# Loading the first batch's state ahead of the weights, and summing it later on VectorE

## The reference

```
# layer 0: cross attention over channels; x_c = x, x_s = context
Mn = Wn @ inorm(x_c) + bn ;  Mm = Wm @ inorm(x_s) + bm
A  = softmax(Mn^T Mm)            # 512 x 512 per batch
x  = Wo @ ((Wl @ x_s + bl) A^T) + bo + x_c
# layer 1: a recurrent block over 128 time steps, 32 heads of 16, state = context
xa = layernorm(x) ; sx = shifted(xa, state row 1) - xa
five mixes of xa and sx -> k, w, v, r, g
s0 = state[:, 2:2+16]            # 32 heads x 16 x 16, the start of the recurrence
out_t = r_t (u * k_t v_t + s) ;  s = k_t v_t + w_t * s
groupnorm(out) * g @ Wo.T + x -> layernorm -> gated feed-forward
```

## Time and profile before

| | us |
|---|---|
| time, median of 3 runs | 1791.22 (1788.71 to 1792.86) |
| time of the execution that was profiled | 1793.89 |
| its span in the trace | 1792.1 |
| PE busy | 1701.1 (95%) |
| DVE busy | 1666.4 (93%) |
| ACT busy | 1183.9 (66%) |
| POOL busy | 1071.3 (60%) |
| mean granted TensorE clock | 0.978 |

### The profile page before, as it was taken

One profiled execution on the slowest core, in us unless ns is written; L12 is line 12 of the kernel. 1 busy time (PEld: TensorE's weight loads), 2 busy tenths in 40 slices (PEclk: granted clock), 3 DMA queues, 4 the chain that ended last, 5 costly groups with the idle time before them and its releaser, 6 DMA issues. The chain is left out here.

```text
span 1792.1 us, 32096 instructions
## 1 busy us (share of the span) xinstructions
PE 1701.1 (95%) x11186; PEld 1185.5 (66%) x11186; DVE 1666.4 (93%) x2259; ACT 1183.9 (66%) x3044; POOL 1071.3 (60%) x816
## 2 busy tenths in 40 slices
PE   3887999999999999999999999999999999999958
PEld 2665776667767666666776667677666767776635
DVE  2279999999999999989999999999999999999993
ACT  1555677667767766766776677677667766775534
POOL 0134667666666676756666666665667666665740
PEclk6898999999999999999999999999999999999989
DMA  6001111101111111011111111111110111110000
GB/s 242 19 30 49 43 43 49 36 31 41 45 49 49 43 46 33 32 43 49 49 43 43 31 36 43 48 49 43 47 34 31 43 49 49 49 37 24 31 18 18
DMA packets 42687, 80.09 MB, mean 45 GB/s; under 512 B 16128, under 2 KB 16512, under 8 KB 41504
## 3 DMA queue, kind: packets, MB, share of 16 engines
q1 hardware_dynamic: 33552, 61.26, 10.2%
q10 hardware_dynamic: 8976, 16.78, 3.1%
HBM read 61.25 MB, written 16.78 MB: 44 GB/s over the span
## 5 line engine op out<-in xcount | busy, mean ns | idle before, releaser
L845 DVE TENSOR_TENSOR_SCAN S<-wrep,S 128x512 f32<-128x512 f32 x256 | 317.4, 1281 | 2.2 <-issue 0.4
L827 DVE TENSOR_TENSOR A<-vrep,kt 128x1008 f32<-128x1008 f32 x256 | 311.9, 1221 | 4.8 <-DMA vrep<-v_dram 4.6
L857 DVE TENSOR_TENSOR A<-S,rt 128x2048 f32<-128x2048 f32 x128 | 292.2, 2283 | 1.1
L522 POOL COPY S<-s 128x16 f32<-128x16 f32 x128 | 118.4, 925 | 256.4 <-DVE A L857 252.7
L489 POOL TENSOR_TENSOR xf<-xf,xa 128x512 f32<-128x512 f32 x160 | 245.2, 1541 | 39.6 <-DVE xf L783 39.5
L1477 ACT ACTIVATE bank<-bank,par 128x128 f32<-128x128 f32 x640 | 173.0, 375 | 57.2 <-PE bank L2066 56.6
L458 POOL TENSOR_TENSOR hrs<-hrs,mhalf 128x32 f32<-128x32 f32 x31 | 189.8, 6123 | 2.6
L456 POOL TENSOR_SCALAR rstd<-mv 128x1 f32<-128x1 f32 (+1 forms) x96 | 84.4, 879 | 164.6 <-DVE mv L717 63.2
L835 DVE TENSOR_TENSOR S<-A 128x1008 f32<-128x1008 f32 x128 | 154.6, 1208 | 2.9
L2109 PE MATMUL bank<-A,head_rep 128*32 128x512 f32 x1024 | 134.1, 616 | 12.1 <-DVE A L857 12.1
L1440 ACT ACTIVATE prob<-bank,nmax 128x512 f32<-128x512 f32 x128 | 87.1, 680 | 83.5 <-DVE nmax L724 83.4
(11 more groups left out here) (162 smaller groups left out, 4187.9 us busy)
## 6 DMA issues: line engine op xcount, KB each, us to landing
vrep<-v_dram SPq DMA_DIRECT2D x64, 512.0 KB
xc<-x_c SPq DMA_DIRECT2D x32, 256.0 KB, 2.6
xs<-x_s SPq DMA_DIRECT2D x32, 256.0 KB, 2.9
v_dram<-vT ACTq DMA_DIRECT2D x32, 256.0 KB
out<-rr ACTq DMA_DIRECT2D x31, 256.0 KB, 2.0
st<-state SPq DMA_DIRECT2D x64, 2.0 KB, 7.4
Wv<-big_w SPq DMA_DIRECT2D x1, 1024.0 KB, 6.5
Wk<-big_w SPq DMA_DIRECT2D x1, 1024.0 KB, 8.5
```

The costliest lines, as they stand in the source:

```text
L827: ve_.tensor_tensor(A[:, u % 2, half * WJ:(half + 1) * WJ, 0:P - 2], vrep[:, half, :, 0:P - 2], k, ALU.mult).then_inc(dve_outer.sem, 1)
L845: last = ve_.tensor_tensor_scan(s, w, s, 0.0, ALU.mult, ALU.add)
L857: ve_.tensor_tensor(out4, s, r, ALU.mult).then_inc(dve_read.sem, 1)
```

## The change

Two calls move. The transfer of s0 of batch 0 is issued in front of the eight weight matrices in place of behind them. On VectorE the sum over it (`mid_s0` of batch 0) goes from its place ahead of `att_rstd` of batch 0 to behind `att_rstd1` of batch 0, some 20 instructions later. Nothing is added or removed, and the waits of each call go with it.

```diff
             def opening():
                 load_x(1, 1)
                 load_st1(0, 0)
+                load_s0(0, 0)
                 load_weights()
                 load_st1(1, 1)
-                load_s0(0, 0)
                 load_s0(1, 1)
...
                 att_stats(*at(0))
                 att_aggr(*at(0))
-                mid_s0(*at(0))
                 att_rstd(*at(0))
                 centre_wv()
                 att_max(*at(0), 0)
...
                 att_xag(*at(0))
                 att_rstd1(*at(0))
+                mid_s0(*at(0))
                 att_stats(*at(1))
```

## The result

| | before | changed |
|---|---|---|
| median of the runs beside each other, us | 1789.97 (4 runs, 1788.06 to 1792.86) | 1769.93 (4 runs, 1768.04 to 1773.54) |
| ratio, with 95% interval | | 0.9889 [0.9866, 0.9912] |
| profiled execution, span | 1793.89, 1792.1 | 1771.42, 1769.6 |
| clock, mean over the span | 0.978 | 0.985 |

The kernel is 20.0 us faster, where 19.3 was forecast: 1769.93 against 1772. The forecast's own range and the wider one both hold it. A ratio is that of the mean times, so it can differ a little from that of the medians.

What follows compares the result with a forecast made beforehand. The opening decides: four engines stand still for 22 us behind one small sum waiting for s0. Terms: -22.0 for the wait, +2.7 for uncovered centring, 0 for the rest, -19.3, so 1772 us (1768.5 to 1775.5).

Steps and rivals of the forecast that it cites:

- the wider one: Whole kernel: 1765 to 1778 us, said to hold about 8 in 10 or a little more.
- The wait that goes: VectorE, before batch 0's first norm: the wait for s0 vanishes, norm at 8.91 in place of 30.91, 22.00 us earlier.
- The centring becomes the limit: VectorE, before the first maximum: centring waits for Wv, landing near 13.1, and ends at 19.3; takes 2.7 us off the gain.
- S0 is ready between 16.6 and 18.6: ScalarE and TensorE chain from norm to first maximum: S0 ready before centring ends at 19.3, even at half clock.
- The 15.7 us behind are unchanged, transfers or not: Batch 0, from first maximum to `att_xin`: still 15.7 us, with no price for running beside the weight transfers.
- The allowance: TensorE and ScalarE beside weight transfers: up to 0.1 us each over a dozen operations, given as 0 to 0.5, taken as 0.
- rival A: TensorE's gap before S2, 0.90 us grown to 2.4: clock falls, giving back up to 3.4 us, 1774.5; chance 0.18.
- The moved sum is hidden: VectorE, second batch's statistics: the sum adds 0.13 us, hidden because ScalarE takes that norm only later.
- No other wait: TensorE's first use of the weights moves from 75.35 to 56, still 25 us after the last landed: no new wait.
- The clock: TensorE, shifted opening: half-clock spells may vanish or be added, about 1 us for a short one, at most 3.4; not summed.
- its own sign, L754 behind 14 us: VectorE, start of the sum over Wv: expected near 13.1; the forecast counts as wrong if it starts after 14.

Runs made afterwards that it cites:

- e5: The changed kernel, unaltered, run again for a second trace beside the kernel before: 1769.81 us, ratio 0.9902.
- e6: The kernel before, unaltered, run again for a second trace: 1787.70 us, ratio 1.0000.
- e1: Against the kernel before, only the transfer of s0 of batch 0 moves ahead of the weights; the sum stays: 1767.41 us, ratio 0.9874.
- e2: Against the kernel before, only the sum over s0 moves to its later place; the transfer stays behind the weights: 1770.95 us, ratio 0.9891.
- e9: Changed kernel plus eleven filler products on TensorE between S1 and S2 of batch 0: 1768.14 us, ratio 0.9894.
- e7: Changed kernel with Wv fetched ahead of the small weights, the centring left in its place: 1768.26 us, ratio 0.9886.
- e8: Changed kernel with the centring of Wv moved behind the last inverse of batch 0, second series: 1766.11 us, ratio 0.9885.
- e11: Changed kernel with late centring, and eight in place of five filler products ahead of batch 0's first multiplications: 1765.45 us, ratio 0.9870.
- e12: Late centring and eight filler products ahead of batch 0's first multiplications once more, for a second set and trace: 1766.32 us, ratio 0.9869.
- e4: Changed kernel with the centring of Wv moved behind the last inverse of batch 0, first series: 1768.97 us, ratio 0.9879.
- e10: Kernel before with the sum over s0 and the centring of Wv both moved later, the transfer left behind the weights: 1768.11 us, ratio 0.9891.
- e3: Kernel before with the transfer of s0 issued behind four of the eight matrices, the sum left in place: 1780.72 us, ratio 0.9946.

## Why the prediction was right

1. *The wait that goes.* 22.00 us at the norm, with the norm at 8.91. In e5 and e6 it moved from 31.39 to 8.91, by 22.5; in the first pair from 30.91 to 10.30, by 20.6, since x and context came late. Right in mechanism, and in size where they came in time.
2. *The centring becomes the limit.* Right: no idle ahead of the first L724 in the first changed trace, e1, e2, e5 and e9, and an earlier first maximum when it is out of the way (e7, e8). The term, what the first maximum gains less than the norm, was set at 2.7. It is 20.6 - 18.1 = 2.5 in the first pair and 22.5 - 19.7 = 2.8 in the second. So the term held, but not its parts. With s0 ahead of it Wv landed at 13.5 to 14.25 and not at 13.06: the one trace that I had, with 12.86, was the earliest of all. This is the input that was mis-sized, and it put the first maximum at 20.0 and 20.5 in place of 19.3. In the first pair x and context were late too, which took from the term what Wv added; in the second the chain from norm to maximum took 8.29 us in the kernel before (e6) and not 7.70. With 7.70 the centring cost 20.00 - (8.91 + 7.70) = 3.4 us in e5, which is what e7 gained. That the errors nearly cancelled was luck. (Between Wv and the pair of s0 stand eight transfers, not nine; the nine steps of 0.50 us are right.)
3. *S0 is ready between 16.6 and 18.6.* The kernels without the centring in the way show it at 16.61, 15.83, 16.23 and 17.53. For the changed kernel itself I estimate it from its L2017, with 1.13 us from the start of that line to the maximum as in e7: 18.65 in the first trace (17.52 + 1.13) and 16.4 in e5. Right, as both are before the centring ends; but the upper end was a little low, as the norm was late, and the lower a little high, as the clock rose earlier in e8 (L2004 3.48 us, 3.78 in the earlier trace rows). In e1, where the norm is at 12.12, the same estimate gives 19.8, only 0.6 us ahead of the limit.
4. *The 15.7 us behind are unchanged, transfers or not.* 15.70 us in the first changed trace, while the weights were still landing, and the same in both of the kernel before, where they had landed. Right, and with it the 0 for TensorE and ScalarE beside heavy transfers. (The allowance was added up wrongly: a dozen operations at up to 0.1 us are up to 1.2 us, not 0.5. As none was paid, nothing hung on it.) Where the way was longer, 16.7 in e5 and 17.2 in e2, it is the slow spell of rival A.
5. *The moved sum is hidden.* From L734 to L766 it takes 5.99 us in the changed kernel, and 6.00 in e1, where the sum isn't there. Right.
6. *No other wait.* L1985 at 56.07; nothing waits for the seven other matrices. Right.
7. *The clock.* It gave back 1.2 us in the second batch of the first pair, and took 1.5 there in the second pair; in the gap it cost 1.0 and 1.5 in two traces (e5, e2). These were in the forecast as spread and not as a sum, and that was the right place for them.

That the measured 20.0 is so near to 19.3 is partly luck: the series on the second chip gives 17.5 by its ratio of 0.9902 and 18.3 by its medians. The two series together bracket the forecast; by the mean of their ratios, 0.9896, the gain is about 18.7. By its own sign, L754 behind 14 us, the forecast was wrong in the first trace (14.30) and not in e5 (13.73): the sign was drawn tighter than the landing of Wv allows. That one half is enough wasn't said: the prediction treated both as one, and priced neither alone. e1 and e2 show that each would do.

## What to carry to other kernels

Look for the instruction behind a long wait, not at the wait: an operation of 0.2 us in a strict queue waited 23 us and cost the kernel some 19, and it was enough to move either it or what it waits for. The gain of such a move isn't the wait but the wait less what was hidden beneath it; find the next instruction with its own late input, here the centring behind Wv, and compute when it ends. Use more than one trace for the landing of a transfer: one matrix landed over a range of 1.4 us in executions of nearly the same program, more than the 1.2 us by which the first maximum was missed. And follow a gain of 1 or 2 us to a milestone some batches on: in e11 and e12 it was there at the first maximum and gone by the fifth batch.

## What the runs showed of the hardware that was not expected

- In these traces the granted clock isn't to be trusted ahead of its first recorded change. From 8 to 40 us the second trace of the kernel before has it at 1.00 throughout, though L2004 took 3.78 us there as at 0.50 in the first. The durations of known matmuls are the better clock: 1.98 us for the four of L2004 at full speed, 3.78 at half. The mean over the span carries the fault: it is 0.978 in the first trace of the kernel before and 0.985 in e6, the same kernel, and the changed kernel's 0.985 counts as full speed the time up to 15 us, in which its L2004 took 3.78 us. So the step from 0.978 to 0.985 in the table of the result isn't shown to be the change's doing.
- TensorE's second filling, five products in ten instructions of 128 columns, takes 1.38 us in some executions (first trace of before, e4, e9, e10) and 2.50 in others (first changed trace, e1 to e3, e5 to e8) of the same instructions. So the clock is up or down there by the execution, before anything that the change can reach on TensorE.
- Transfers issued first also vary: the first batch's context was awaited for 0 to 1.43 us in the fourteen traces, with the same two transfers ahead of its pair.
